# Cross-attention of a perceiver block: transposes and products moved two slots behind the scores, scores in three banks, sums through memory, five places for key stacks

## What is computed

```python
def _L0_xattn_ref(query_antecedent, memory_antecedent, bias, Wq, Wk, Wv, Wo):
    h = NUM_HEADS                                   # 16 heads of depth 32
    q = _split_heads(query_antecedent @ Wq, h) * d_head ** (-0.5)
    k = _split_heads(memory_antecedent @ Wk, h)
    v = _split_heads(memory_antecedent @ Wv, h)
    logits = jnp.einsum('bhqd,bhkd->bhqk', q, k) + bias
    weights = jax.nn.softmax(logits, axis=-1)
    x = jnp.einsum('bhqk,bhkd->bhqd', weights, v)
    b, _, l, d = x.shape
    x = x.transpose(0, 2, 1, 3).reshape(b, l, h * d)
    return x @ Wo
...
x = x + _L0_xattn_ref(_layernorm(x, axis=-1), ctx_1024, fside_1x1xSxS2_0, Wq, Wk, Wv, Wo)
x = x + _L0_attn_ref(_layernorm(x, axis=-1), ...)   # recurrence, ternary weights
x = x + _L0_ffn_ref(_layernorm(x, axis=-1), ...)    # experts, the best two of eight
```

## Time and profile before

| | us |
|---|---|
| median of three runs | 1223.56 |
| lowest, highest | 1220.26, 1224.00 |
| the profiled execution | 1225.35 |
| span of its instructions | 1223.60 |

### The profile page before, as it was taken

The page is one execution under the profiler, slowest core; times in us unless marked ns, Lnnn a source line. Parts: engine busy times, 40 slices in busy tenths (PEclk is TensorE's granted clock), DMA queues, the critical chain, the costliest instruction groups (busy, mean ns, idle before and its releaser), DMA issues. The chain is left out here.

```text
span 1223.6 us, 17246 instructions
## 1 busy us (share of the span) xinstructions
PE 1039.0 (85%) x7041; PEld 798.5 (65%) x7046; DVE 532.6 (44%) x901; ACT 418.2 (34%) x552; POOL 210.7 (17%) x207
## 2 busy tenths in 40 slices
PE   5979986999876989986999988743757999999996
PEld 4748655788655778665788666422325999977774
DVE  4232566272565263566352566378764211111110
ACT  1011564251664235465231466145631111111110
POOL 0022241002241001322001321144221010011000
PEclk9979998999998989999899999966875999999998
DMA  7103865423865323775222775800004998699910
GB/s 274 35 1 97 183 150 142 145 79 112 181 143 149 147 114 107 169 158 141 82 98 86 164 159 118 328 1 0 1 2 128 387 376 290 227 369 314 312 19 11
DMA packets 87255, 183.48 MB, mean 150 GB/s; under 512 B 11800, under 2 KB 19992, under 8 KB 86400
## 3 DMA queue, kind: packets, MB, share of 16 engines
q1 hardware_dynamic: 85056, 177.49, 48.0%
q0 software_dynamic: 2112, 4.80, 1.7%
HBM read 117.92 MB, written 14.00 MB: 108 GB/s over the span
## 5 line engine op out<-in xcount | busy, mean ns | idle before, releaser
L714 ACT ACTIVATE prob<-prob,top 128x2048 f32<-128x2048 f32 x64 | 128.5, 2008 | 54.9 <-DVE top L554 54.9
L400 PE MATMUL psum<-ident,prob 128*128 128x128 f32 x1024 | 138.9, 281 | 9.1 <-ACT prob L714 7.4
L400 PEld LDWEIGHTS psum<-ident,prob 128*128 128x128 f32 x1024 | 121.0, 144 | 30.0 <-ACT prob L714 10.0
L322 PE MATMUL psum<-ctx_part,wk_hi 128*128 128x512 f32 x256 | 105.1, 411 | 34.6 <-POOL ctx_part L808 19.3
L1543 PE MATMUL psum<-xT,wring 128*128 128x128 f32 (+3 forms) x1024 | 133.5, 291 | 0.6 <-ACT xT L1831 0.6
L1543 PEld LDWEIGHTS psum<-xT,wring 128*128 128x128 f32 x1024 | 131.4, 193 | 2.8 <-issue 1.9
L676 ACT COPY kT<-psum 128x512 f32<-128x512 f32 x64 | 37.6, 587 | 256.6 <-PE psum L324 256.6
L554 DVE CUSTOM_DVE_ANT_0 prob<-psum,biasmap,top 128x1024 f32<-128x1024 f32 x64 | 82.2, 1284 | 79.3 <-PE psum L385 79.3
L797 POOL CAST keys_hi<-kT 128x1024 fp32r<-128x1024 f32 x32 | 33.3, 1040 | 477.3 <-ACT kT L676 308.8
L554 DVE CUSTOM_DVE_ANT_0 prob<-psum,biasmap 128x1024 f32<-128x1024 f32 x64 | 78.2, 1222 | 82.7 <-PE psum L385 82.5
L323 PE MATMUL psum<-ctx_part,wk_hi 128*128 128x512 f32 x256 | 103.2, 403 | 0.0
(11 more groups left out here) (226 smaller groups left out, 1401.0 us busy)
## 6 DMA issues: line engine op xcount, KB each, us to landing
wring<-in_w SPq DMA_DIRECT2D x64, 1024.0 KB, 9.7
stack<-keys_hi SPq DMA_DIRECT2D x192, 128.0 KB, 2.4
ctx_raw<-in_ctx_t SPq DMA_DIRECT2D x16, 1024.0 KB, 5.4
stack<-keys_lo SPq DMA_DIRECT2D x96, 128.0 KB, 2.4
early_stack<-keys_hi SPq DMA_DIRECT2D x64, 128.0 KB, 2.4
ternary<-ternary_weights SPq DMA_DIRECT2D x1, 6272.0 KB, 24.6
prob<-in_w_gate_t SPq DMA_DIRECT2D x1, 5632.0 KB, 17.6
early_stack<-keys_lo SPq DMA_DIRECT2D x32, 128.0 KB, 2.4
```

The lines of the kernel that those rows point to most:

```text
L322: pe.matmul(psum[:, w, :], wh, ctx_part[:, half, 0, k, :], start=(k == 0), stop=False)
L400: mm = pe.transpose(psum[:, w + i, j * P:(j + 1) * P], prob[:, prob_slot(n, j), kt * P:(kt + 1) * P], ident[:, :])
L714: act.activation(prob[:, slot, :], prob[:, slot, :], ACT.Exp, bias=top[:, h, 1:2], scale=-1.0, accum_out=top[:, h, 2:3]).then_inc(*raised. ...
```

## The change

- **Slots.** `score_slot` writes units of 512 keys into banks 0, 1, 2 in turn, and `add_bias` works on such units. Transposes come two slots behind (`TURN_LATER`), products two steps behind their transposes (`WEIGH_LATER`); ten steps (`TAIL`) follow a batch's last scores. The filler tiles of the first quad are dealt out by `FILLERS` over ten slots. VectorE moves pairs 3 and 7, ScalarE the rest. Pairs use banks 3 to 6, the output bank 7.
- **Stacks.** Five places in a ring; two lie in kT (key_stack), whose first two tiles are then no longer needed. The three copies of a head are 256 KB each, in halves only for the first head of quads 0 and 1. GpSimd waits for all stacks of the quad before, both halves, ahead of its first half.
- **First quad's keys** are split by VectorE (`split_first_keys`), and so is the whole of each context chunk.
- **Sums.** Inverse sums go to memory as 4 by 128 and come back spread over 128 partitions (`store_sums`, `load_sums`), both on SyncE's queue ahead of the next quad's stacks.
- **Border.** Only one key tile of the next batch stands before the last product.
- **Ternary.** `mean_at` is two tiles later, and with it rounding and store.
- **Start.** `normalise_x` comes behind the second value tile.

```diff
-MOVED_BY_VECTOR = (1, 5, 7)
+MOVED_BY_VECTOR = (3, 7)
+UNITS = KEYS // CHUNK
+SLOTS_OF_QUAD = QUAD * HALVES
+TURN_LATER = 2
+WEIGH_LATER = 2
+FILLERS = (2, 2, 1, 2, 1, 2, 1, 2, 2, 1)
...
-        self.mean_at = self.sum_at + len(self.sums) + 1
+        self.mean_at = self.sum_at + len(self.sums) + 3
...
+        RING_PLACES = (stack[:, 0, :], key_stack[:, 0, :], key_stack[:, 1, :], stack[:, 1, :], stack[:, 2, :])
...
-        work = Ring((2, 3, 4, 5))
-        OUT_BANKS = (6, 7)
+        work = Ring((3, 4, 5, 6))
+        quad_out = psum[:, 7, 0:P]
...
-            def score_half(n, j, half):
+            def score(n, j, c):
...
+                if c % 2 == 0:
+                    pe.wait_ge(*stack_landed(n, j, c // 2))
+                if (n, j, c) >= (0, 0, 3):
+                    pe.wait_ge(*biased.at(*unit_before(n, j, c, 3)))
...
+                work.restart()
+                for t in TAIL:
+                    turn_and_weigh(b, t, t - WEIGH_LATER)
+                multiply_pair(*pair_of_step(b, STEPS - 2))
+                if b + 1 < B:
+                    project_key_tile(b + 1, 0, 0)
...
+                multiply_pair(*pair_of_step(b, STEPS - 1))
...
+            def split_first_keys(b):
+                n = DT * b
+                dve.wait_ge(*values_projected.at(b, VTILES * (CHUNKS - 1) - 1))
+                dve.wait_ge(*ctx_split.at(CHUNKS * b + CHUNKS - 1))
+                dve.wait_ge(*keys_copied.at(b, CHUNKS - 1, 0))
+                for half in range(HALVES):
+                    keys = slice(half * HALF, (half + 1) * HALF)
+                    dve.tensor_copy(keys_hi[:, keys], kT[:, 0, keys]).then_inc(*keys_high_v.made(n, half))
+                    dve.wait_ge(*keys_high_v.at(n, half))
+                    dve.tensor_tensor(keys_lo[:, keys], kT[:, 0, keys], keys_hi[:, keys].bitcast(F32),
+                                      ALU.subtract).then_inc(*keys_low_v.made(n, half))
...
+                last = DT * (b + 1) - 1
+                move_pair(last - 1, LAST)
+                invert_sums(last)
+                finish(last - 1)
                 if b + 1 < B:
                     split_chunk(CHUNKS * (b + 1))
+                for p in MOVED_BY_VECTOR:
+                    move_pair(last, p)
...
                 pool.wait_ge(*keys_copied.at(b, CHUNKS - 1, g))
+                for j in range(QUAD):
+                    for half in range(HALVES):
+                        pool.wait_ge(*stack_landed(n - 1, j, half))
                 for half in range(HALVES):
                     keys = slice(half * HALF, (half + 1) * HALF)
-                    for j in range(QUAD if g else 0):
-                        pool.wait_ge(*stack_landed(n - 1, j, half))
...
+            def store_sums(n):
+                sp.wait_ge(*sums_inverted.at(n))
+                sp.dma_start(sums_dram[n].rearrange("j t -> t j"), rinv[:, n % 2, :],
+                             allow_slow_non_contiguous=True).then_inc(*sums_stored.made(n))
+
+            def load_sums(n):
+                sp.wait_ge(*sums_stored.at(n))
+                if n >= 1:
+                    sp.wait_ge(*weighted.at(n - 1))
+                source = sums_dram[n].rearrange("j (o t) -> j o t", o=1).broadcast_to([QUAD, DH, P])
+                sp.dma_start(rT[:, :], source).then_inc(*sums_in.made(n))
```

More of the change, by code:

```diff
@@ L305, in projected_tiles, with fillers @@
             return [(*one, tile) for tile, one in enumerate(order)]
+        def fillers(b):
+            tiles = [("values", VTILES * (CHUNKS - 1) + t) for t in range(1, VTILES)] + [("keys", DT - 1)]
+            steps, at = [(tile, k) for tile in tiles for k in range(DT)], 0
+            for count in FILLERS:
+                yield steps[at:at + count]
+                at += count
+            assert at == len(steps)
         def tensor_attention(pe):
@@ L490, in most_attention @@
[L490 to L495 removed]
+                project_value_tile(b, VTILES * (CHUNKS - 1))
+                beside = fillers(b)
+                for n in range(DT * b, DT * (b + 1)):
+                    for i in range(SLOTS_OF_QUAD):
+                        score_slot(n, i)
+                        for (kind, which), k in next(beside, ()):
+                            if kind == "values":
+                                project_value_tile(b, which, (k,))
+                            else:
+                                project_key_tile(b, CHUNKS - 1, which, (k,))
+                        if n > DT * b:
+                            turn_and_weigh(b, *steps_of_slot(n, i))
```

410 lines of the change are left out of this document (187 added, 223 removed).

## The result

The changed kernel takes 1264.31 us (median of 4 runs, 1256.39 to 1270.27) where the kernel before took 1222.82 beside it: a ratio of 1.034, 95% interval 1.027 to 1.041. Forecast were 1199 and a range of 1168 to 1222. The profiled execution took 1270.27 (span 1268.5, mean granted clock 0.903 against 0.932 before). Behind the attention nothing moved: 433 us against 436. All of the loss lies in the attention, which ends at 837.0 instead of 789.1.

A forecast was written before the change was run, and what follows sets the result against it. The ring of GpSimd's split and stack copies was taken to bound the quads. Start -9.5, batches -4.9, -6.1, -7.1 and +2.7 sum to -24.9: 1225.35 becomes 1200.4, the median 1.8 lower, so 1199 us; range 1168 to 1222.

The forecast's parts named there:

- part 4: Border between batches: GpSimd's 6.7 us wait goes; batch interval 176.3 us, including 1.5 for the clock and 1.0 for sums.
- 1.0 for the sums: Inverse sums written to memory between stack copies: 1.0 us a batch, bounds 0 and 2.4 a quad.
- Rival C: Slower: sums' small writes hold DMA engines between stack copies; 1227 us at 4 us each, 1235 at 5; chance 0.08.
- step 1: Program start: normalise_x behind the second value tile makes a TensorE stretch 17.9 instead of 28.5 us, net -9.5.
- Ring: GpSimd's split, stack copies, next split: still sets the quads, period 21.1 us, no better than before.
- rival B: Stack copies of 256 KB move at twice the rate, so the ring does not bind: 1128 us, chance 0.08.
- Slots and borders: TensorE's half-head slots take 2.15 us in quad 3; GpSimd's 6.7 us wait at the batch border goes.
- step 5: Batch 2: the later ternary store delays the early stacks and the whole ring with them, +8.0 us.

The follow-up runs named there:

- sums on TensorE: Changed kernel with the inverse sums spread on VectorE and turned on TensorE again instead of going through memory: 1206.62 us, ratio 0.987.
- half-stack kernel: Kernel with the sums on TensorE, every head's stack copied in two 128 KB halves and split half by half: 1165.82 us, ratio 0.954.

## Why the prediction was wrong, step by step

**The step that failed is in part 4**, "1.0 for the sums", with "bounds 0 and 2.4 a quad" and "I take the low side, since the bytes are 2 KB". Batch 0, with and without the memory's way (changed kernel against sums on TensorE): last score 91.3 against 81.4 us after the first, tail and projections 104.9 against 98.0; together 16.8 us for a term of 1.0, of which 6.9 lie behind the last score, where the prediction put nothing. Over the attention it is 837.0 - 776.6 = 60.4. Not only the value, both bounds were too low. The nearest row was a copy between on-chip buffers in rows of 4 KB, which says nothing on how long small pieces take to land in memory. And the term was priced by its bytes, when the trace has the engines idle and the price is 7.8 to 11.4 us of waiting for completion, with SyncE's queue behind it and stretches at half rate after it.

**Rival C had the cause, half of the mechanism, and its number by luck.** It put 7 us a batch on the time for 4 us a store, on two quads of each of the four batches, and said that it decides from 3 us. At the 8.5 to 9.6 of batch 0 the same formula gives 1199 + 8 x 8 to 9 = 1263 to 1271. That this meets 1264.31 is luck: the formula puts the whole price on the ring, 16 us a batch, where batch 0 lost 9.9 ahead of its last score and 6.9 behind it, and it stands on a sum that comes out too low without the store as well (below). It reckoned with 4 and 5 us a store and was given 0.08. It named only DMA engines that are held, and they show a busy share of 0.00; the runs show that the in-order wait on SyncE and the held completions both carry it, and that on ScalarE's queue the store takes away the first and lengthens the second.

**Right, by their own steps:**
- Start: 11.4 us against the 9.5 of step 1 (whose own terms, 28.5 - 17.9 - 1.3, give 9.3). In the timeline TensorE's projection of the queries starts at 63.65 after a wait of 0.83.
- Ring: GpSimd's splits are released by stack DMAs, and without the sums' way come 21.9 and 22.0 us apart (said: 21.1). 256 KB copies land in 5.0 us at the median and 198 to 217 GB/s, so rival B fell. Of the two places of the Trainium skill that the prediction names, the ports of SBUF — State Buffer, section Door 1: The DMA port swizzle (by its figures an estimate of 218 GB/s), agree with this. The fit of DMA: Bandwidth & Descriptors, section Anatomy of one DMA, does not give it; the page states it for DMAs issued by GpSimd, and these are issued by SyncE, several at a time.
- Slots and borders: scores of quad 3 stand at 193.05, 195.17, 197.28 (2.11 us apart, said 2.15), and the 6.68 us of the earlier trace rows have no successor.
- The late ternary store: issued at 493.27, first stack copy at 502.45. TensorE loses 3.85 us before the first score and 3 to 4 more in the ring behind it, near the 8.0 of step 5.

**The rest of the sum.** With the sums on TensorE the attention ends at 776.6, where the steps without their 1.0 a batch give about 760. The 16 us are: intervals of batch 0 and the last batch 4 longer each than the steps without that 1.0 (179.4 and 118.2), batches 1 and 2 together 9.6 (184.4 and 183.8), start 1.4 back. In batch 0 and in the last all of it sits ahead of the end of quad 3's slots, which comes 83.6 and 83.0 us after the first score instead of 79.0: the ring's period is 22 us instead of 21.1. Beside it TensorE ran at half rate while quad 1 waited for its stacks, a stretch of the kernel with the sums on TensorE:
```profile
129.50:137.50 8.00, 5.64 (x16) 3.67 (x15) 3.04 (x11) 2.58 (x3) 0.00 (x0) 0.50 1.01 217
```
The copies fill the DMA engines there, so I had called such slow work harmless; whether it is was not separated.

**What the ring could still give** was not asked: GpSimd waits for all four whole stacks in the changed kernel, and I noted that as a given. Undoing it was worth 40.8 us, more than the rest of the change without the memory's way (1206.6 against 1221.5 of the kernel before beside it).

## What to carry to other kernels

Price a new DMA by when its completion comes and by who stands behind the wait for it, not by its bytes or by the engines' busy share; if no row shows a store of that shape (piece size and neighbours in memory), its upper bound is open and belongs in the range. Before values go transposed to memory in 4-byte pieces, lay them so that each partition writes 16 bytes in one piece (the run here stored them so but read them back in the wrong order, and no correct kernel of this kind was built), or keep them on chip. Where a resource is used in a ring (split, copy, score, split), hand it on in halves: a step that seems hidden may only be lying beside another wait, so test it again after each fix.

## What the hardware did that I had not expected

- 128 or 512 pieces of 4 bytes, written side by side into memory by 128 partitions, complete 7.2 to 11.4 us after their issue; while the 512 were awaited the DMA engines showed 0.00 busy. 512 such pieces 64 bytes apart: 2.0 us in the first quad; 16 bytes apart 3.4; 128 pieces of 16 bytes side by side 3.0. The time follows the number of pieces in the same stretch of memory.
- Such a store holds back completions of other DMAs, on another queue too: a stack copy whose bytes were moved by 142 us landed at 148.5 instead of 142.5, and a 64 KB store took 10 us to land.
- A wait of 9 us on TensorE cost more than itself: the 19.6 us behind it ran at a mean granted clock of 0.86. In the half-stack kernel, where the scores of the stretch from 143 to 200 waited 0.7 to 2.0 us, it was 1.00.
